# Phase 2 mask moved from TensorE to the maxima's instruction, router tables in PSUM, maxima 16 steps ahead, and other steps for squares, norms, scalings and expert loads

## What is computed

```python
xn = rms_norm(x, g_norm) * (1 + scale) + shift            # scale, shift = emb @ W_emb + b_emb
q, k, v = heads(xn @ W_qkv)                                # 16 heads of 32
o = softmax(rms(q) @ rms(k).T * 32 ** -0.5) @ v            # no mask
y = o + o @ W_out
...
h = y + attention(rmsnorm(y))                              # q, k: 16 plain + 16 rotary, causal mask
out = h + moe(rmsnorm(h))                                  # 1 shared expert, top 2 of 7 by sigmoid
return x + out
```

## Time and profile before

| | us |
|---|---|
| median of 3 runs | 1332.19 |
| lowest, highest | 1326.33, 1333.14 |
| the profiled execution | 1329.95 |
| its span | 1328.2 |
| PE, DVE, ACT, POOL busy | 1197.7, 741.2, 576.2, 289.6 |
| granted TensorE clock, mean of the span | 0.966 |

### The profile page before, as it was taken

One profiled execution on the slowest core, in us unless ns is written; L12 is line 12 of the kernel. 1 busy time (PEld: TensorE's weight loads), 2 busy tenths in 40 slices (PEclk: granted clock), 3 DMA queues, 4 the chain that ended last, 5 costly groups with the idle time before them and its releaser, 6 DMA issues.

```text
span 1328.2 us, 18938 instructions
## 1 busy us (share of the span) xinstructions
PE 1197.7 (90%) x6315; PEld 854.4 (64%) x6315; DVE 741.2 (56%) x1550; ACT 576.2 (43%) x1248; POOL 289.6 (22%) x242
## 2 busy tenths in 40 slices
PE   5979999999999899999999989989988898999970
PEld 5845555655566366567777657766656787888860
DVE  6565675477545765654564564475444775444433
ACT  3324364345434554554554544354354752222210
POOL 1313122101210221001012101100124454555530
PEclk9969999999999999999999999999999998999995
DMA  6054243134213632441464354265358533666669
GB/s 248 32 175 127 65 143 111 48 98 161 86 48 95 209 88 77 164 136 49 158 209 120 125 171 127 81 214 159 89 202 297 183 95 84 110 110 112 111 128 332
DMA packets 88127, 178.44 MB, mean 134 GB/s; under 512 B 12609, under 2 KB 23265, under 8 KB 86497
## 3 DMA queue, kind: packets, MB, share of 16 engines
q1 hardware_dynamic: 79216, 156.90, 37.0%
q0 software_dynamic: 8512, 19.93, 8.5%
q10 hardware_dynamic: 304, 0.40, 0.1%
HBM read 110.86 MB, written 65.27 MB: 133 GB/s over the span
## 4 chain that ended last, share of the span: by engine, by line
PE 77%; DVE 9%; ACT 4%; DMA 4%; issue 4%; SPq 1%; POOL 0%; ACTq 0%; DVEq 0%; POOLq 0%
PE psum L852 14%; PE psum L667 9%; PE psum L668 8%; PE psum L669 8%; PE psum L836 7%; PE psum L812 6%; PE psum L676 3%; PE psum L930 3%; PE psum L932 3%; PE psum L931 3%; DVE nmax L1570 2%; PE psum L957 2%; PE psum L959 2%; PE psum L958 2%; PE psum L899 2%
## 5 line engine op out<-in xcount | busy, mean ns | idle before, releaser
L1164 ACT ACTIVATE probs<-psum 128x512 f32<-128x512 f32 (+3 forms) x512 | 256.4, 516 | 238.9 <-PE psum L839 126.1
L1570 DVE TENSOR_REDUCE nmax<-psum 128x1 f32<-128x512 f32 (+3 forms) x512 | 289.5, 584 | 109.6 <-PE psum L812 76.3
L836 PE MATMUL psum<-stack 97*128 97x512 f32 (+3 forms) x512 | 204.0, 399 | 21.4 <-ACT probs L1164 18.5
L852 PE MATMUL psum<-probs,vals 128*33 128x512 f32 (+3 forms) x1024 | 212.4, 537 | 0.0
L812 PE MATMUL psum<-stack 96*128 96x512 f32 (+3 forms) x512 | 209.3, 413 | 2.0 <-DMA stack<-split 1.2
L836 PEld LDWEIGHTS psum<-stack 97*128 97x128 f32 x512 | 98.9, 193 | 43.1 <-ACT probs L1164 27.5
L812 PEld LDWEIGHTS psum<-stack 96*128 96x128 f32 x512 | 99.6, 195 | 35.0 <-issue 23.2
L852 PEld LDWEIGHTS psum<-probs,vals 128*33 128x33 f32 x1024 | 49.9, 112 | 101.8 <-issue 71.3
L667 PE MATMUL psum<-w_hi,xh 128*128 128x512 f32 (+1 forms) x256 | 95.4, 373 | 4.2 <-DVEq L1437 2.6
L668 PE MATMUL psum<-w_hi,xl 128*128 128x512 f32 (+1 forms) x256 | 93.7, 366 | 0.0
L669 PE MATMUL psum<-w_lo,xh 128*128 128x512 f32 (+1 forms) x256 | 93.6, 366 | 0.0
(11 more groups left out here) (235 smaller groups left out, 2360.9 us busy)
## 6 DMA issues: line engine op xcount, KB each, us to landing
stack<-split_s SPq DMA_DIRECT2D x378, 128.0 KB, 3.1
split_s<-split SPq DMA_DIRECT2D x64, 512.0 KB, 2.8
xt<-in_x_dram SPq DMA_DIRECT2D x4, 1024.0 KB, 5.3
x_s<-yt SPq DMA_DIRECT2D x4, 1024.0 KB, 5.0
xt<-x_s SPq DMA_DIRECT2D x4, 1024.0 KB, 4.8
yt<-in_x_dram SPq DMA_DIRECT2D x4, 1024.0 KB, 5.5
res<-x_s SPq DMA_DIRECT2D x4, 1024.0 KB, 8.8
acc_s<-yt SPq DMA_DIRECT2D x4, 1024.0 KB, 6.0
```

What stands on the lines that cost most here:

```text
L836: last = nc.tensor.matmul(psum[:, bank, lo:S], st[:, 1, t * P:(t + 1) * P], st[:, 0, lo:S], start=True, stop=not causal)
L852: nc.tensor.matmul(psum[side:side + VW, o.bank(p), lo:S], vals[k % 2][:, t, h, :], probs[:, M % NX, lo:S], start=(t == 0), stop=(t == NT - ...
L1164: sk.cleared(nc.scalar.activation(probs[:, M % NX, lo:S], psum[:, sk.bank(M), lo:S], ACT.Exp, scale=SCALE), M)
L1570: sq.cleared(V.tensor_reduce(nmax[:, M // STEPS_P % 2, c:c + 1], psum[:, sq.bank(M), 0:n], AX.X, ALU.max, negate=True), M)
```

## The change

- **Mask.** `scores` no longer issues the mask product. In phase 2 `maximum` is a tensor_tensor_reduce: it adds scores and a table `causal` (0 or -1e30, 128x512 in SBUF, written by POOL at the start), writes the negated sum back to PSUM, and accumulates its minimum. `scores_t` keeps its mask product.
- **Maxima.** `LEAD` is 16; the turn of the maxima stays at the same step (`TURN_AHEAD` 5).
- **Steps.** In `beside_heads` square, norm and scale of batch k + 2 go to other steps (24 to 29 for k = 1 and 2, with norm and scale as before; 14 to 39 for k of 3 and more), and square2 to router as well.
- **Tables.** In the tile phase `hit`, `prob`, `slot_e` and a copy of `upto` lie in PSUM bank 0. `rope` and `rwt` lie elsewhere, `ones` is set by DVE in the last batch.
- **Experts.** SP loads expert 2 after shared tile 0, 4, 5, 6 one slot or two later, expert 0 after tile 8 and not first. ACT's pieces are listed ahead of and behind `shared_out`. POOL takes (6, 2) from DVE, waits only before (3, 2), (2, 0) and (2, 1), and issues the first two gathers behind all of its pieces. DVE's (0, 0) goes ahead of `hidden` in slot 13, (0, 1) and (0, 2) to the end of slot 13.

```diff
-LEAD = 14
+LEAD = 16
+TURN_AHEAD = 5
...
-            put((26, 30, 34, 38), each("square2", i, NT))
-            put((39, 40, 41, 42), each("norm2", i, 4))
-            put((43, 44, 45, 46), each("scale2", i, NT))
-            put((47, 49, 51, 53), each("x2", i, NC))
-            put((55, 59), each("router", i, 2))
+            put((28, 33, 36, 41), each("square2", i, NT))
+            put((43, 43, 44, 44), each("norm2", i, 4))
+            put((47, 47, 49, 49), each("scale2", i, NT))
+            put((51, 52, 54, 55), each("x2", i, NC))
+            put((59, 62), each("router", i, 2))
...
-        put((40, 41, 42, 43), square)
-        put((44, 45, 46, 47), norm)
-        put((51, 52, 53, 54), scale)
+        if phase(j) == 1:
+            put((40, 41, 42, 43) if k == 0 else (24, 25, 28, 29), square)
+            put((44, 45, 46, 47), norm)
+            put((51, 52, 53, 54), scale)
+        else:
+            put((14, 16, 20, 22), square)
+            put((26, 27, 28, 30), norm)
+            put((31, 35, 36, 39), scale)
...
-    p, m = divmod(M + LEAD - STEPS_P - 1, STEPS_P)
+    p, m = divmod(M + TURN_AHEAD, STEPS_P)
...
-BY_DVE = ((6, 2), (0, 0), (0, 1), (0, 2))
+BY_DVE = ((0, 0), (0, 1), (0, 2))
...
+        side = psum[:, 0, :]
+        hit = side[:, 0:NT * NROUTED].rearrange("p (j n) -> p j n", n=NROUTED)
+        upto_p = side[:, 160:160 + P]
+        prob = side[:, 288:288 + B * NT * NE].rearrange("p (j e) -> p j e", e=NE)
+        slot_e = side[:, 288:288 + B * NT * NE].rearrange("p (j e) -> p j e", e=NE)
...
-            load_expert(0)
             ring.wait_full(sp, ("out", LAST, NT - 1))
             load_expert(3)
             store_acc(LAST)
-            load_expert(2)
             store_x2(LAST)
...
-                if causal:
-                    last = nc.tensor.matmul(psum[:, bank, t * P:n], mask[:, :], identr[:, :], start=False, stop=True)
-                sq.filled(last, M)
+                sq.filled(nc.tensor.matmul(psum[:, sq.bank(M), 0:n], st[:, 0, t * P:(t + 1) * P], st[:, 1, 0:n],
+                                           start=True, stop=True), M)
...
-                if (e, c) in POOL_SLOT:
-                    pool.wait_ge(h_hi, POOL_SLOT[e, c] + 1)
-                if (e, c) == (6, 0):
-                    get_rows()
+                if (e, c) in ((3, 2), (2, 0)):
+                    pool.wait_ge(h_hi, {(3, 2): 4, (2, 0): 5}[e, c] + 1)
+                if (e, c) == (2, 1):
+                    pool.wait_ge(g_step, STEP_SLOTS)
                 split_expert(e, c)
+            get_rows()
...
+                if phase(k) == 1:
+                    sq.cleared(V.tensor_reduce(out, psum[:, sq.bank(M), :], AX.X, ALU.max, negate=True), M)
+                else:
+                    x = psum[:, sq.bank(M), 0:(t + 1) * P]
+                    sq.cleared(V.tensor_tensor_reduce(out=x, in0=x, in1=causal[:, (NT - 1 - t) * P:], scale=-1.0, scalar=-NEG,
+                                                      op0=ALU.add, op1=ALU.min, accum_out=out), M)
...
             def choose_first():
 
+                glink(V.tensor_copy(upto_p, upto[:, :]))
...
+                if s == READ_SLOT + 1:
+                    split_expert(0, 0)
                 if s + 1 < NTILES:
                     hidden(s + 1)
...
                 if s == READ_SLOT + 1:
-                    split_expert(6, 2)
-                    split_expert(0, 0)
-                if s == READ_SLOT + 2:
                     split_expert(0, 1)
                     split_expert(0, 2)
```

More of the change, by code:

```diff
@@ L332, in build @@
         ssh = rest("ssh", [P, NT, 2 * H])
+        rope = rest("rope", [P, 2, NT, RD])
+        rwt = yt[:, 0, 0:NC * NE].rearrange("p (c e) -> p c e", e=NE)
         vrow = junk[:, 0:P]
-        wemb = at("w_emb", rest.where - 4 * (NT * 2 * H + S + 2 * NC * S), [P, NC, 2 * D])
+        wemb = at("w_emb", rest.where - 4 * (2 * NT * RD + NT * 2 * H + S + 2 * NC * S), [P, NC, 2 * D])
         last_ = Strip(WEIGHTS_AT)
@@ L350, in build @@
         top = work("top", [P, 2, B * NT, NE])
-        prob, tied = work("router_probs", [P, B * NT, NE]), work("router_ties", [P, B * NT, NE])
-        slot_e = work("slot_by_expert", [P, B * NT, NE])
+        tied = work("router_ties", [P, B * NT, NE])
         counts = [work(f"counts{i}", [P, 8 + B * NT, NE]) for i in range(3)]
-        work.where -= 4 * (8 + B * NT) * NE
-        hit, load = work("tile_hit", [P, NT, NROUTED]), work("tile_payload", [P, 2, NT, PAY, NROUTED], F32R)
+        work.where = last_.where - ew_size * 2 * NR + 4 * 2 * NT * P
+        load = work("tile_payload", [P, 2, NT, PAY, NROUTED], F32R)
         payload = work("payload", [P, 2, B * NT, PAY])
@@ L364, in build @@
         part = work("part", [P, 2, 2, B * NT])
+        ones = work("ones", [P, P])
         upto, tok1 = work("upto", [P, P]), work("token_plus_1", [P, B * NT])
@@ L782, in beside @@
                 elif kind == "upto":
+                    pe.wait_ge(ones_ok, 1)
                     ring.wait_free(pe, key)
@@ L807, in scores @@
                 sq.wait_free(pe, M)
-                causal = phase(k) == 2
-                n = (t + 1) * P if causal else S
-                bank = sq.bank(M)
+                n = (t + 1) * P if phase(k) == 2 else S
                 st = stack[0:XSTACK, :, h % NSTK]
-                last = nc.tensor.matmul(psum[:, bank, 0:n], st[:, 0, t * P:(t + 1) * P], st[:, 1, 0:n],
-                                        start=True, stop=not causal)
-                if causal:
-                    last = nc.tensor.matmul(psum[:, bank, t * P:n], mask[:, :], identr[:, :], start=False, stop=True)
-                sq.filled(last, M)
+                sq.filled(nc.tensor.matmul(psum[:, sq.bank(M), 0:n], st[:, 0, t * P:(t + 1) * P], st[:, 1, 0:n],
+                                           start=True, stop=True), M)
             def turn_max(p):
@@ L831, in scores_t @@
                 sk.wait_free(pe, M)
-                causal = phase(k) == 2
-                lo = t * P if causal else 0
+                masked = phase(k) == 2
+                lo = t * P if masked else 0
                 bank = sk.bank(M)
@@ L836, in scores_t @@
                 last = nc.tensor.matmul(psum[:, bank, lo:S], st[:, 1, t * P:(t + 1) * P], st[:, 0, lo:S],
-                                        start=True, stop=not causal)
-                if causal:
+                                        start=True, stop=not masked)
+                if masked:
                     last = nc.tensor.matmul(psum[:, bank, lo:lo + P], identr[:, :], mask[:, :], start=False, stop=True)
@@ L1232, in _ @@
                     beside(("x2", LAST, 3))
-                pieces = [(e, c) for at_, e, c in HI_SLOT if s == at_]
-                for e, c in pieces[:1]:
+                for e, c in HI_EARLY.get(s, ()):
                     split_expert(e, c)
@@ L1240, in _ @@
                     nc.scalar.activation(tied[:, :, :], logits[:, :, :], ACT.Exp, scale=-1.0).then_inc(g_exp, 1)
-                for e, c in pieces[1:]:
+                for e, c in HI_LATE.get(s, ()):
                     split_expert(e, c)
@@ L1567, in maximum @@
                 sq.wait_full(dve, M)
-                n = (t + 1) * P if phase(k) == 2 else S
                 c = h % 2 * NT + t
-                sq.cleared(V.tensor_reduce(nmax[:, M // STEPS_P % 2, c:c + 1], psum[:, sq.bank(M), 0:n], AX.X, ALU.max,
-                                           negate=True), M)
+                out = nmax[:, M // STEPS_P % 2, c:c + 1]
+                if phase(k) == 1:
[4 more added lines that the diff above has]
+                                                      op0=ALU.add, op1=ALU.min, accum_out=out), M)
             for n in range(2):
@@ L1617, in _ @@
                             beside(key)
+                    if k == LAST and m == 1:
+                        ring.wait_full(dve, ("v", LAST, NT - 1))
+                        V.memset(ones[:, :], 1.0).then_inc(ones_ok, 1)
             def lo_of_x(i):
```

43 lines of the change are left out of this document (24 added, 19 removed).

## The result

The changed kernel takes 1291.43 us (median of 4 runs, 1289.41 to 1300.0) against 1330.38 us for the kernel before: ratio 0.9722, 95% interval 0.967 to 0.9774. It is 39 us faster, where the forecast added up 48.7 and named 1283. The value lies in the range of 1270 to 1300, but outside the forecast's own 1277 to 1288, and on the numbers that two rivals gave (1292 and 1291). So the direction needs no explanation; the missing 8 to 10 us do.

What follows compares the result with a forecast made beforehand. PE, busy 90% of the span, was taken to bound the kernel. Gains of 24 + 5 + 3.5 + 3 - 0.5 + 13.7 = 48.7 us gave 1283 us, within 1277 to 1288; wider range 1270 to 1300.

Steps and rivals of the forecast that it cites:

- Part 1: 256 mask products of the maxima pass no longer issued on PE: 24 us gained, bounds 15.4 and 29.4.
- Rival 1: A mask is worth only its 0.06 us, or ACT gives the rest back: 9 us less, 1292; chance 0.16.
- Part 2: Phase 2 maxima by tensor_tensor_reduce: 0.15 us each, 38 us of DVE work, hidden beside PE, cost 0.
- Rival 3: The tensor_tensor_reduce is slow and DVE binds phase 2; 1377 us at 1.0 us more per maximum; chance 0.03.
- Part 3: Moved steps and earlier maxima remove PE gaps: 5, 3.5 and 3 us, with 0.5 us against.
- (a): Part 3: moved squares end PE's waits before L836, 5 us; Part 4: tile_rows loaded first, 4.4 us.
- (b): Part 3: x2 transposes stop waiting for scalings, 3.5 us; Part 4: router chain freed from POOL contention, 3.2 us.
- (c): Part 3: maxima 16 steps ahead, 3 us; Part 4: DVE's splits no longer meet POOL's, 7.1 us, minus 1.
- Part 4: Shared tiles: PE's waits for rows, router chain and expert splits shrink, 13.7 us gained.
- Rival 2: Shared tiles get a new wait for the old one, PE at half clock: 8 us less, 1291; chance 0.13.
- Rival 4: Moved steps collide and gaps simply move, so parts 3 and 4 give half: 1294; chance 0.08.

Runs made afterwards that it cites:

- e1: Changed kernel with the mask product back on TensorE and the maxima plain reduces again: 1309.81 us, 17.6 us slower than the changed kernel.
- e5: Changed kernel with the mask product back on TensorE but VectorE's masked maxima kept: 1310.6 us, 20.1 us slower than the changed kernel.
- the five profiles: Profiles with the same step code: the changed kernel, its rerun e6, e9, e10 and e11; late steps 412.3, 411.6, 412.4, 404.5 and 406.1 us.
- e3: Changed kernel with squares, norms, scalings, x2 and router at the steps of the kernel before: 1303.71 us, 11.6 us slower than the changed kernel.
- e9: Changed kernel with POOL's old order of expert splits and (6, 2) back on DVE: 1300.48 us, 7.1 us slower than the changed kernel.
- e10: Changed kernel with experts 0 and 2 loaded ahead of the first tiles' rows again: 1297.73 us, 4.3 us slower than the changed kernel.
- e11: Changed kernel with the router's four small tables in SBUF instead of PSUM, POOL's new order kept: 1304.18 us, 10.8 us slower than the changed kernel.
- e6: Control: the changed kernel run again unchanged, 1290.54 us against 1329.88 us for the kernel before, ratio 0.9705.

## Why the prediction was right, and where it missed

**Part 1, the mask product: right in mechanism, mis-sized at its end.** The late successor, 0.12 us a mask in a burst, is there (e1), and the total of PE work is 22.3 us, between the bounds of 15.4 and 29.4; the loss against 29.4 is the masks at other places, worth some 0.07 us each. But I took off only 29.4 - 24 = 5.4 us for everything, and let it come back "before L836" from ACT's exponentials. Of the 22.3 us, the late steps kept 425.6 - 412.3 = 13.3 by e1 and 428.9 - 411.6 = 17.3 by e5 (14 to 18 without the clock); by the medians the part is worth 17.6 to 20.1. ACT's exponentials gave back 2.8 us as I argued (0.9 to 3.7); what I had not thought of is that the maxima (2.7) and the stack's loads (1.7, and 0.4 to 1.7 over the five profiles) would give back as much and more, as they too were just in time for the longer steps. This is the term that was off: 24 should have been some 14 to 20. Rival 1 came near the time, with the giving back, though not with its 0.06 us a mask.

**Part 2: right.** The instruction is 12 ns longer than the reduce at 512 columns, with 140 ns of accumulator read: the 0.15 us each that I took. As the read runs beside the next instruction, DVE is at 246 of 413 us and not at 273. PE's waits for a free score bank did not come as such; the 2.7 us of waits for maxima at L825 are gone with the product back and the new instruction kept (0.2 in e5), so they too are PE's speed. Rival 3 has nothing for it.

**Part 3: right in sum by e3 (8.5 forecast for (a) and (b), 11.6 measured), but not by its own reckoning.** I had added up the gaps of before that the edit would remove. The gaps at the squares fell from 1.38 to 0.76, not to nothing: all waits for the exponentials from 18.5 to 15.5 us, 3 of the 5 that I took. The gap at x2 only changed its name, from `res` (1.62) to `split` (2.06). And yet e3 costs 11.6, and the late steps without the clock 7 to 9, since the old steps are worse under a faster PE. Taken out one at a time, product (17.6), steps (11.6), lead (3.5) and tiles (14.5) make 47 us where all together bring 39. That looks as if product and steps shared one slack that is counted twice, but it is not shown: each of these terms has some 5 us of chance to each side, and without the clock the late steps add up plainly. The product brings 13.8 us with the old steps (before against e3) and 14 to 16 with the new ones, the new steps 7.0 with the old product (before against e1) and 7 to 9 without it, and both together 21 to 23. That 47 is near my 48.7 is chance. What is shown is simpler: with either set of steps some 7 of the product's 21 to 22 us come back as gaps (25.8 to 33.0, and 18.9 to 26.4). (c) The lead: 3 forecast, 0 to 5 measured, undecided. I wrote that the stack's load was hidden, and "if it were not, PE would wait at L812": it does, 3.8 us in two places, since I reckoned with its issue and landing (3.1 us) alone and not with what is ahead of it in the queue: 2 MB of residuals for the wait at 907.07, seven loads of phase 2's weights for the one of 1.54 us at 446.65. And of the gap of 1.01 us at 157.23 nothing was won, as the wait for `qk` took its place.

**Part 4: right in size, 13.7 forecast and 14.5 measured** (from the last step to the last tile; e9 and e10 make 11.4 by their medians). (a) 4.4 against 4.8 in e10. (b) and (c) 3.2 + 7.1 - 1 = 9.3 against 9.5 in e9, though the stall near the routed tiles came there from splits that end late and hardly from DVE's meeting POOL's. The clock is 1.00 from slot 0 to the routed tiles, and the wait of ACT's (0, 0) costs PE 0.36 us, not 1. But I gave the PSUM tables a price of their own. Without them the new order of POOL would lose 15.9 us by the trace (10.8 by the medians), about all that part 4 gains: the tables pay by making the order possible, and what they would bring under the old one, 14.5 - 4.8 - 9.5 = 0.2 us, can't be told from nothing. The pair 1.71 and 0.28 us, which I set beside the rule on two SBUF inputs, can't show what an operand in PSUM does, as L1651 reads SBUF twice as well and only comes after POOL's split; e11 shows it. Rival 2 did not come about. Rival 4 (parts 3 and 4 give half) is true of part 3 alone.

**Sum by part, forecast and measured:** mask 24 and 14 to 20; steps, lead and prologue 11 (5 + 3.5 + 3 - 0.5) and, beside the other parts, what is left of the span's 39.1: 39.1 - 14.5 - 17.3 = 7.3 with e5's 17.3 for the mask, 4.5 with the 20.1 of its median; tiles 13.7 and 14.5. How the last few us divide stays open: in the late steps the clock's part alone moved by 7 us between profiles of the same code. So the time lies 8 us from the forecast for reasons that the gaps show in part (some 7 us that came back in the late steps, where I had taken off 5.4 in all, and gaps of part 3 that moved on), and on the side of the range where rivals 1 and 4 stood.

## What to carry to other kernels

When a change makes the bounding engine faster and also moves the work of the others, don't book the saved time in full: here a third of it came back as gaps, because the others were just in time for the longer step. Check for every engine and queue what it must deliver per step. And before reading anything from the length of one profile, compare profiles of the same code: here gaps and work repeated within 2 us and the lost clock did not within 7. Before counting on a small load, list the large ones ahead of them on the same queue. Here an order of work that lets POOL run without pauses beside DVE paid only while the DVE instructions beside it read one operand from PSUM.

## What was not expected of the hardware

- A DVE instruction of 0.63 us stands still for 2.1 us beside a POOL split of 2.4, and so do the next ones, one after another: eight of L1741 took 1683 ns in the mean with both inputs in SBUF.
- A stall of PE can cost more than itself: 3.02 us of waiting and 1.7 of lost clock at 993.66 of e10; 2.27 and 3.25 at 907.07 of after. But the same code does not always pay it. A wait of 2.06 us at the x2 transposes of batch 5 stands in each profile of the changed steps; the 6.5 us behind it had a granted clock of 0.74 in after, 0.52 in e6, 0.54 in e9 and 1.00 in e10. So a single profile doesn't tell what a stall costs in clock. What decides was not tried.
- The accumulator read of a masked maximum is listed with 140 ns, and 256 of them with 35.9 us, yet with the product back (e5 against e1) they and the longer instruction together cost 3.3 us by the late steps and 2.5 by the medians, neither of them clear of chance.
